# Softmax over graph edges: segmented maxima by scans over four heads at once, the first pass moved behind each row's scores, links between rows on GpSimd

## The reference

```
score = einsum('ehc,ehc->eh', q[dst], k[src]) / sqrt(32)   # edges x 4 heads
m     = segment_max(score, dst)
p     = exp(score - m[dst])
alpha = p / maximum(segment_sum(p, dst)[dst], 1e-16)
out   = segment_sum(v[src] * alpha[:, :, None], dst)
```

## Time and profile before

| what | value |
|---|---|
| time, median of 3 runs | 5352.15 us (5348.26 to 5366.02) |
| profiled execution, its own time | 5363.49 us |
| its span | 5361.2 us |
| TensorE / VectorE busy share | 81% / 66% |
| ScalarE / GpSimd busy share | 42% / 52% |
| `softmax_rows`, first to last instruction | 2578.01 to 2612.98 us |
| `softmax_weights`, first VectorE instruction to last | 2614.36 to 2696.58 us |

### The profile page before, as it was taken

One profiled execution on the slowest core, in us unless ns is written; L12 is line 12 of the kernel. 1 busy time (PEld: TensorE's weight loads), 2 busy tenths in 40 slices (PEclk: granted clock), 3 DMA queues, 4 the chain that ended last, 5 costly groups with the idle time before them and its releaser, 6 DMA issues. The chain is left out here.

```text
span 5361.2 us, 99690 instructions
## 1 busy us (share of the span) xinstructions
PE 4333.2 (81%) x24044; PEld 3651.3 (68%) x24045; DVE 3546.1 (66%) x7926; ACT 2271.4 (42%) x4136; POOL 2789.6 (52%) x2733
## 2 busy tenths in 40 slices
PE   6666777777667676767388749999999999999998
PEld 3555555554344444444177549999999999999998
DVE  5888888886778888878776674444445654444444
ACT  2333333433255555555156544444444443344333
POOL 1777777771377777777021114444444443344433
PEclk8888888888877787777699869999999999999999
DMA  3444444442567777766145443433434442233332
GB/s 101 116 116 117 117 116 117 118 117 58 155 192 199 198 203 200 197 194 194 33 141 155 119 127 144 147 145 144 156 137 164 173 147 109 97 145 139 134 128 94
DMA packets 543941, 750.81 MB, mean 140 GB/s; under 512 B 58756, under 2 KB 442755, under 8 KB 543528
## 3 DMA queue, kind: packets, MB, share of 16 engines
q1 hardware_dynamic: 461976, 521.43, 29.0%
q0 software_dynamic: 81552, 224.63, 15.6%
HBM read 584.41 MB, written 161.45 MB: 139 GB/s over the span
## 5 line engine op out<-in xcount | busy, mean ns | idle before, releaser
L2395 PE MATMUL ps<-moving,parts 128*128 128x384 f32 (+1 forms) x11662 | 2015.5, 331 | 38.7 <-ACT moving L2457 20.4
L548 POOL DMA_INDIRECT arena<-table_kv,arena x1664 | 1739.1, 1045 | 581.4 <-issue 506.0
L2395 PEld LDWEIGHTS ps<-moving,parts 128*128 128x128 f32 x11662 | 1949.2, 188 | 72.3 <-ACT moving L2457 29.4
L2336 POOL CAST moving<-counts 128x1152 fp32r<-128x1152 uint8 (+1 forms) x420 | 477.2, 1136 | 737.6 <-PE ps L2395 607.0
L344 ACT ACTIVATE counted<-ps 128x392 uint8<-128x392 f32 x1568 | 666.4, 502 | 350.9 <-PE ps L335 305.4
L2336 POOL CAST moving<-big 128x1152 fp32r<-128x1152 uint8 (+1 forms) x413 | 469.5, 1137 | 608.9 <-PE ps L2395 608.9
L335 PE MATMUL ps<-by_place,by_lo 128*128 128x392 bf16 x1568 | 631.5, 525 | 127.7 <-DVE by_place L299 101.6
L658 PE MATMUL ps<-arena 128*128 128x137 f32 x1664 | 326.5, 353 | 333.1 <-DVE arena L792 324.4
L2457 ACT ACTIVATE moving<-counts 128x1152 fp32r<-128x1152 uint8 (+1 forms) x360 | 366.9, 1024 | 435.4 <-PE ps L2395 432.6
L2457 ACT ACTIVATE moving<-big 128x1152 fp32r<-128x1152 uint8 (+1 forms) x354 | 360.4, 1023 | 429.6 <-PE ps L2395 429.5
L658 PEld LDWEIGHTS ps<-arena 128*128 128x128 f32 x1664 | 278.5, 243 | 364.2 <-ACT arena L703 217.5
(11 more groups left out here) (332 smaller groups left out, 5237.1 us busy)
## 6 DMA issues: line engine op xcount, KB each, us to landing
counts<-adjacency SPq DMA_DIRECT2D x53, 2352.0 KB, 8.5
big<-adjacency SPq DMA_DIRECT2D x52, 2352.0 KB, 8.5
adjacency<-slots SPq DMA_DIRECT2D x784, 98.0 KB
edge_values<-arena SPq DMA_DIRECT2D x208, 256.0 KB, 3.2
arena<-edge_values SPq DMA_DIRECT2D x208, 256.0 KB, 3.2
arena<-table_kv,arena POOLq DMA_INDIRECT x1664
big<-table_norm SPq DMA_DIRECT2D x60, 192.0 KB, 5.7
big<-adjacency SPq DMA_DIRECT2D x7, 1568.0 KB, 6.5
```

Of the source, the lines that this page charges most:

```text
L548: pool.indirect_dma_start(m.ring4[r][:, k * 2 * D:(k + 1) * 2 * D], None, table, bass.IndirectOffsetOnAxis(m.src[:, j * HALF + k:j * HALF ...
L2336: pool.tensor_copy(to, of).then_inc(by_pool, 1)
L2395: mm = pe.matmul(m.bank(g % 2, n * P), d.parts[SOURCE[u]][:, s + q, t_, :], moving[:, q * n * P:(q + 1) * n * P], start=(s + q == 0 and t_ ...
```

## The change

- The links are written for all four heads at once (in two areas, rows 0 to 3 and rows 4 to 6), with -1e30 also at each head's first element, so that one scan of 128x512 covers a row's four heads. `fwd` and `bwd` are gone. A row's forward scan writes `seg`, and its backward scan runs over `seg` in place, so that `seg` then holds the maximum in both directions.
- The first pass and the building of the links move to `softmax_rows`. A row's two scans follow its copy to `srow`, and that copy moves from VectorE to ScalarE.
- What depends on `dst` alone (ends, their transposes, their copies, `cont`, `single`, `onward`, `backward`, `penalty`) moves to `softmax_rows` too: GpSimd gathers, TensorE transposes in row 1, ScalarE copies in row 2, and GpSimd works out the 4x896 rows, with subtract, square and add in place of compare and multiply.
- In `softmax_weights` the maxima brought back by TensorE are not scan starts any more. Two small max instructions, with PSUM as an input, put them into the first and last element of each row of `seg`, and the second pass is again two scans of 128x512 a row, then the subtraction. The seven max are gone. ScalarE does the copies to `weight`, each behind the next row's exponential.
- `weight` moves from column 9000 to 9376 of its buffer.

```diff
@@ constants and Memory.shared @@
+WEIGHT_AT = 9376
-        self.fwd = split(big[:, 2 * SC:3 * SC], ROWS, H1, P)
-        self.bwd = split(big[:, 0:SC], ROWS, H1, P)
-        self.weight = big[:, 9000:9000 + SC]
+        self.seg = split(big[:, 0:SC], ROWS, H1, P)
+        self.weight = big[:, WEIGHT_AT:WEIGHT_AT + SC]
+        self.links = [(range(0, 4), big[:, 2 * SC:2 * SC + 4 * H1 * P + 1]), (range(4, ROWS), hits[:, 0:(ROWS - 4) * H1 * P + 1])]
+        self.linked_to = split(self.weight[:, 0:ROWS * (P - 1)], ROWS, P - 1)
...
@@ softmax_rows and its helpers @@
+class SoftmaxParts:
+
+
+    def __init__(self, m):
+        row = lambda t, a=0: t[0:H1, a:a + COLS]
+        flat = [t.rearrange("p a k n -> p (a k n)") for t in (m.hit, m.hitT, m.msg)]
+        self.first_dst, self.last_dst = row(m.stage_b), row(m.stage_c, COLS)
+        self.cont, self.single = row(m.stage_d), row(m.stage_d, COLS)
+        self.onward, self.backward, self.penalty = (row(t) for t in flat)
+        self.last_max, self.first_max = row(m.stage_a), row(m.stage_b)
+        self.ends = m.small[:, 0:ROWS * 4 * H1].rearrange("p (j q h) -> p j q h", q=4, h=H1)
...
+def run_onward(dve, m, j, of):
+
+    links, at = links_of(m, j)
+    flat = lambda t: t[:, j].rearrange("p h e -> p (h e)")
+    return dve.tensor_tensor_scan(flat(m.seg), links[:, at:at + H1 * P], flat(of), -BIG, ALU.add, ALU.max)
+
+
+def run_backward(dve, m, j):
+
+    links, at = links_of(m, j)
+    seg = m.seg[:, j].rearrange("p h e -> p (h e)")[:, ::-1]
+    return dve.tensor_tensor_scan(seg, links[:, at + H1 * P:at:-1], seg, -BIG, ALU.add, ALU.max)
+
+
 def softmax_rows(nc, m, ct):
 
-    with Phase(nc, "sr1", "turned copied placed taken vec") as (block, turned, copied, placed, taken, vec):
+    with Phase(nc, "sr1", "turned copied placed taken vec linked onward backward dated dates_turned dates_rowed chain") as (
+            block, turned, copied, placed, taken, vec, linked, onward, backward, dated, dates_turned, dates_rowed, chain):
         by_step = m.score.rearrange("p (s h) -> p h s", h=H1)
         turned_scores = m.stage_c[:, 0:H1 * P]
         turned_picks = m.stage_a[:, 0:2 * P]
+        dst = m.dst_rows[:, :].rearrange("p (j e) -> p j e", e=P)
+        parts = SoftmaxParts(m)
 
         @block.tensor
         def _(pe):
@@ -1218,6 +1256,13 @@
                     pe.transpose(m.bank(0)[:, h * P:(h + 1) * P], by_step[:, h, c], m.ident[:, :])
                 pe.transpose(m.bank(1)[:, 0:P], m.pick0[:, c], m.ident[:, :])
                 pe.transpose(m.bank(1)[:, P:2 * P], m.pick1[:, c], m.ident[:, :]).then_inc(turned, 1)
+                if j == 1:
+                    pe.wait_ge(dated, 2)
+                    for q in (2, 3):
+                        for i in range(ROWS):
+                            mm = pe.transpose(m.ps[0:H1, 1024 * q + i * P:1024 * q + (i + 1) * P], parts.ends[:, i, q, :],
+                                              m.ident[:, :])
+                        mm.then_inc(dates_turned, 1)
                 pe.wait_ge(copied, 2 * (j + 1))
                 if j >= 2:
                     pe.wait_ge(taken, j - 1)
@@ -1229,19 +1274,64 @@
 
         @block.scalar
         def _(act):
+            def take(j):
+                act.wait_ge(placed, min(2 * (j + 2) - 1, 2 * ROWS - 1))
+                act.activation(m.srow[:, j], m.bank(2 + j % 2).rearrange("p (h e) -> p h e", h=H1), ACT.Copy).then_inc(taken, 1)
+
             for j in range(ROWS):
                 act.wait_ge(turned, j + 1)
                 if j:
                     act.wait_ge(placed, 2 * j - 1)
                 act.activation(turned_scores, m.bank(0), ACT.Copy).then_inc(copied, 1)
                 act.activation(turned_picks, m.bank(1, 2 * P), ACT.Copy).then_inc(copied, 1)
+                if j:
+                    take(j - 1)
+                if j == 2:
+                    for q, to in ((2, parts.first_dst), (3, parts.last_dst)):
+                        act.wait_ge(dates_turned, q - 1)
+                        act.activation(to, m.ps[0:H1, 1024 * q:1024 * q + COLS], ACT.Copy).then_inc(dates_rowed, 1)
+            take(ROWS - 1)
+
+        @block.gpsimd
+        def _(pool):
+            p = parts
+            pool.tensor_copy(p.ends[:, :, 2, :], copies(dst[:, :, 0], 2, H1)).then_inc(dated, 1)
+            pool.tensor_copy(p.ends[:, :, 3, :], copies(dst[:, :, P - 1], 2, H1)).then_inc(dated, 1)
+            pool.memset(p.cont[:, 0:1], 1.0).then_inc(chain, 1)
+            pool.memset(p.backward[:, COLS - 1:COLS], 1.0).then_inc(chain, 1)
+            pool.wait_ge(dates_rowed, 2)
+            pool.tensor_tensor(p.cont[:, 1:COLS], p.first_dst[:, 1:COLS], p.last_dst[:, 0:COLS - 1], ALU.subtract).then_inc(chain, 1)
+            pool.tensor_tensor(p.single, p.first_dst, p.last_dst, ALU.subtract).then_inc(chain, 1)
+            pool.wait_ge(chain, 4)
+            pool.tensor_tensor(p.cont, p.cont, p.cont, ALU.mult).then_inc(chain, 1)
+            pool.tensor_tensor(p.single, p.single, p.single, ALU.mult).then_inc(chain, 1)
+            pool.wait_ge(chain, 6)
+            pool.tensor_tensor(p.onward, p.cont, p.single, ALU.add).then_inc(chain, 1)
+            pool.tensor_tensor(p.backward[:, 0:COLS - 1], p.cont[:, 1:COLS], p.single[:, 0:COLS - 1], ALU.add).then_inc(chain, 1)
+            pool.wait_ge(chain, 8)
+            for to, of in ((p.onward, p.onward), (p.backward, p.backward), (p.penalty, p.cont)):
+                pool.tensor_scalar(to, of, -BIG, -BIG, ALU.mult, ALU.max).then_inc(chain, 1)
 
         @block.vector
         def _(dve):
+            for some, links in m.links:
+                n = len(some) * H1 * P
+                dve.memset(links[:, 0:n].rearrange("p (a e) -> p a e", e=P)[:, :, 0:1], -BIG).then_inc(linked, 1)
+                dve.memset(links[:, n:n + 1], -BIG).then_inc(linked, 1)
+            dve.tensor_tensor(m.linked_to, dst[:, :, 1:P], dst[:, :, 0:P - 1], ALU.is_equal).then_inc(linked, 1)
+            dve.wait_ge(linked, 5)
+            for some, links in m.links:
+                n = len(some) * H1 * P
+                dve.tensor_scalar(links[:, 0:n].rearrange("p (j h e) -> p j h e", h=H1, e=P)[:, :, :, 1:P],
+                                  copies(m.linked_to[:, some[0]:some[0] + len(some)], 2, H1), -1.0, BIG,
+                                  ALU.add, ALU.mult).then_inc(linked, 1)
             places_of_blocks(dve, m, ct, vec)
+            dve.wait_ge(linked, 7)
             for j in range(ROWS):
-                dve.wait_ge(placed, min(2 * (j + 2) - 1, 2 * ROWS - 1))
-                dve.tensor_copy(m.srow[:, j], m.bank(2 + j % 2).rearrange("p (h e) -> p h e", h=H1)).then_inc(taken, 1)
+                dve.wait_ge(taken, j + 1)
+                run_onward(dve, m, j, m.srow).then_inc(onward, 1)
+                dve.wait_ge(onward, j + 1)
+                run_backward(dve, m, j).then_inc(backward, 1)
...
@@ softmax_weights @@
+            dve.tensor_copy(p.ends[:, :, 0, :], m.seg[:, :, :, P - 1]).then_inc(ends, 1)
+            dve.tensor_copy(p.ends[:, :, 1, :], m.seg[:, :, :, 0]).then_inc(ends, 1)
+            for q, to in enumerate((p.last_max, p.first_max)):
                 dve.wait_ge(turned, q + 1)
                 dve.tensor_copy(to, m.ps[0:H1, 1024 * q:1024 * q + COLS]).then_inc(rowed, 1)
...
+            dve.wait_ge(rowed, 2)
+            dve.tensor_tensor_scan(p.onward, p.onward, p.last_max, -BIG, ALU.add, ALU.max).then_inc(chained, 1)
+            dve.tensor_tensor_scan(p.backward[:, ::-1], p.backward[:, ::-1], p.first_max[:, ::-1], -BIG,
+                                   ALU.add, ALU.max).then_inc(chained, 1)
...
+            dve.tensor_tensor(m.seg[:, :, :, 0], m.seg[:, :, :, 0], carried[:, :, 0, :], ALU.max).then_inc(opened, 1)
+            dve.wait_ge(opened, 1)
+            dve.tensor_tensor(m.seg[:, :, :, P - 1], m.seg[:, :, :, P - 1], carried[:, :, 1, :], ALU.max).then_inc(opened, 1)
+            dve.wait_ge(opened, 2)
+
+            def run(j):
+                run_onward(dve, m, j, m.seg).then_inc(onward, 1)
+                dve.wait_ge(onward, j + 1)
+                run_backward(dve, m, j).then_inc(backward, 1)
...
+                run(j)
+                dve.wait_ge(backward, j + 1)
+                dve.tensor_tensor(m.srow[:, j], m.srow[:, j], m.seg[:, j], ALU.subtract).then_inc(shifted, 1)
...
+            def store(j):
+                act.wait_ge(drawn, j + 1)
+                act.activation(m.weight[:, j * P * H1:(j + 1) * P * H1].rearrange("p (s h) -> p h s", h=H1),
+                               m.bank(1 + j % 2).rearrange("p (h s) -> p h s", h=H1), ACT.Copy).then_inc(stored, 1)
+
...
+                if j:
+                    store(j - 1)
+            store(ROWS - 1)
```

More of the change, by code:

```diff
@@ L237, in shared @@
             at += n
-        self.x_scratch = split(self.q[:, 5000:5000 + ROWS * (P + 1)], ROWS, P + 1)
     def bank(self, k, n=512):
@@ L1247, in softmax_weights @@
 def softmax_weights(nc, m):
[L1253 to L1272, removed]
```

(28 more changed lines are left out.)

52 lines of the change are left out of this document (15 added, 37 removed).

## The result

The changed kernel takes 5323.41 us (median of 5 runs, 5312.76 to 5325.56), against 5352.79 us (5 runs, 5348.26 to 5366.02): ratio 0.9942, 95% interval 0.9931 to 0.9953. That is 29.4 us faster, where 29.5 were forecast. Five more runs, against nine of the kernel before on the same chip, gave 5317.52 against 5352.89 us, 35.4 us less: ratio 0.9935 (0.9921 to 0.9949).

What follows compares the result with a forecast made beforehand. VectorE's serial list was taken to bound `softmax_weights`, a TensorE-ScalarE-TensorE loop `softmax_rows`. Saving 43.8 us and losing 14.3 gave 29.5 us: 5352.15 - 29.5 = 5322.7 us, own range 5318 to 5327, with rivals 5306 to 5334.

Steps and rivals of the forecast that it cites:

- The lock between scans and GpSimd's two-input instructions: In `softmax_rows`, VectorE's scans and GpSimd's instructions take turns, never overlapping; the phase then ends at 49.3 us, against 35.0.
- Rival 1: In `softmax_rows`, scans run beside GpSimd unhindered; the phase takes about 35.3 us, the kernel 5308.7 us; chance 0.22.
- Rival 2: In `softmax_rows`, GpSimd's four waits or some 20 engine turns cost 10 us more; kernel 5333 us; chance 0.10.
- Rival 3: GpSimd's nine instructions in `softmax_rows` are much dearer; at 8 us each the kernel takes 5377 us, slower; chance 0.03.
- GpSimd's 17.1 and VectorE's 16.4 us are then served one after another: In `softmax_rows` from 15.8 us on, links and scans add without gap: 15.8 + 33.5 = 49.3 us.
- Both count 0: Changed semaphore clearing around `softmax_rows` and the shift of `weight` by 376 columns were each taken to cost nothing.

## Why the prediction was right

**What one VectorE list says.** In the changed kernel VectorE has no gap worth counting in `softmax_rows`, so the phase is a sum. Its links and `places_of_blocks` end at 16.3 us undisturbed, the 14 scans take 16.7 us (with GpSimd silent), and what GpSimd costs it is the rest. By the timelines above, the stretch is 1.81 us for line 1034 and 1.79, 1.30, 1.41, 1.71 and 1.80 us for five scans, 9.8 in all for six two-input instructions. Three tensor-scalar ones take 0.55, 0.66 and 0.55 us, 1.8 in all. The sum is 16.3 + 16.7 + 9.8 + 1.8 = 44.6 us. With the last term out it is 42.8 (measured 42.85). With 5.8 in place of 11.6 it is 38.8 (measured 38.8).

**Right, point by point.** `softmax_weights`: 38.7 against 38.4, with three misses that nearly cancel. ScalarE's copy takes 1.07 us, where I chose 0.7, and TensorE's last row takes 2.1 (2645.42 to 2647.51), where I chose 2.4; the last subtraction starts 0.25 us later than forecast, for rows are 3.12 us apart and not 3.08. The lock between scans and GpSimd's two-input instructions, taken over from the earlier trace rows, holds for the scan too, and with four partitions in use. Rival 1, scans unhindered, is out by the experiment without links: it would have been 36 us. Rival 2, more waits than work, is out too: the turns cost less than the two engines' work in a row, not more. Rival 3 has no ground: GpSimd's nine instructions last 3.1 us on average beside the scans, under the 5.2 each at which the gain was to be gone. The Trainium skill's rule, page "SBUF — State Buffer", section "Who interferes with whom", agrees with three of the pairs seen here: two-input against two-input instructions, the links of edges against VectorE's tensor-scalar instructions (0.61 to 2.19 us), and a GpSimd cast against a two-input instruction of VectorE (0.56 to 1.47 us). For the second pair the rule asks that VectorE's instruction use both of its port pairs, which the trace does not show, though 0.61 us for 896 elements, against 1.08 for a two-input instruction of that length, fits. For the fourth pair, GpSimd's tensor-scalar instructions on 4x896 against a scan, the measurement decides: 0.6 us lost to an instruction of 3.25 us.

**Off in size.** The term that was mis-sized is "GpSimd's 17.1 and VectorE's 16.4 us are then served one after another". VectorE lost 11.6 us to GpSimd and not 17.1. Six two-input instructions cost it 1.6 us each, not 2.1: alone the squares take 1.67 us and the others 2.07, and about 0.3 us of each does not shut VectorE out (2.07 against losses of 1.71 to 1.81, 1.67 against 1.30 and 1.41). The tensor-scalar ones cost it 0.6, not 1.5, though they last 3.25 us alone and 4.1 beside scans, not 1.5. Here two errors met: too short an instruction and too strict a lock. That left 44.6 us instead of 49.3, below the bounds that I gave (47.6 to 51.1). The lower bound should have allowed for one-input instructions that block little, which I had priced in rival 1 at 5318. That case is 49.3 - 4.5 = 44.8 us for the phase, nearer to the 44.6 measured than the forecast's own term, though these instructions are not free (1.8 us).

**The agreement of 29.5 and 29.4 us is partly luck.** The phases together give 33.8 us. The barrier in front costs 0.4 more and the one between the phases 0.15 less, so the traces give 33.5, or 32.4 with the trace in which GpSimd ended the phase. The interval of the first ratio allows 25 to 37 us, and the second set of runs gave 35.4 us. So by the traces the forecast was 3 to 4 us too low, and that the first median fell on 29.4 is chance. "Both count 0" for the semaphores was nearly so: the way into `softmax_rows` grew from 3.33 to 3.74 us with seven more to clear, and the way out shrank from 1.38 to 1.23 with two fewer. With the two put back, in the run with the first pass in `softmax_weights`, it is 1.38 again (GpSimd's end at 2613.94 to 2615.32).

## What to carry to other kernels

Moving work from VectorE to GpSimd is no cover when both have two-input instructions: here 5.8 us of VectorE's own work became 11.6 us of waiting. Price such a move as GpSimd's duration, nearly in full, added to VectorE's list, and put it where VectorE is idle. What did pay was position: the first pass behind each row (9.2 us), and the exponential, products and copies under the second pass (the copies alone 4.9 us). The work that depends on the dates alone, taken off a serial phase, saved 8.1 us there (from the copies of the ends to the scans over 4x896 it was 12.8 us, 2634.03 to 2646.82, and is 4.7, 2609.86 to 2614.52). But on GpSimd its arithmetic cost `softmax_rows` 8.5 us (44.6 against 36.1 without it), so as the kernel was changed this part gained nothing; on VectorE it costs 2.7 (38.8 against 36.1), and only there does the move pay. The wider scans by themselves gave 1.0 us in the first pass. In the second, 14 wide scans take 17.6 us (7 x 2.52) where 56 narrow ones took 21.2, and most of that is the start no longer read from memory: with it narrow scans were 0.375 us apart, without it 0.315. No run tries that by itself. Where the times of a kernel scatter by 10 us, compare the phases in the traces, not the runs, and look which engine ends each phase.

## What the runs showed of the hardware that was not expected

- A GpSimd tensor-scalar instruction on 896 elements with multiply and max takes 3.25 us alone; with add and multiply, beside scans, 1.8 us. On 128 partitions, 2032 elements with add and multiply take 2.13 us.
- A one-input GpSimd instruction holds VectorE up for some 0.6 us or until it ends. Tensor-scalar instructions on 4x896 cost a scan 0.55 to 0.67 us and a scalar-tensor-tensor 0.63, whether they last 4.1 us or 1.8. Ones on 128 partitions, and a cast on 128, shut out a tensor-scalar (0.61 to 2.19 us) and a two-input instruction (0.56 to 1.47 us) until they end. The number of partitions differs between the two groups and may be the reason; it was not tried by itself.
- Two-input GpSimd instructions on four partitions shut scans out nearly as long as they last: 1.7 to 1.8 us of 2.07.
- The way from one phase to the next grew by 0.41 us with seven more semaphores to clear, and shrank by 0.15 us with two fewer: some 0.06 to 0.07 us each. One run bears on it: with the two put back the second way is again as long as before (1.38 us), though that run also ends its phase with GpSimd, which gave 1.26 us with two fewer.
